# Barriers between the blocks of a two-layer graph network: with and without POOL's drain

## The chip, the cores and the metric

The program runs on one core of one Trainium2 chip. The metric is the device time of one execution in microseconds (us); a lower time is better. Three executions of the kernel before took 2250.91, 2253.52 and 2253.49 us, with a median of 2253.49 us. One more execution was taken with the hardware profiler, and all rows below are from that one.

Engine names as in the profile: PE is TensorE, DVE is VectorE, ACT is ScalarE, POOL is GpSimd, SP is SyncE. A name with a q behind it (POOLq, SPq) is the engine's own instruction queue: it runs waits, semaphore updates, branches and drains, and it hands the engine's work to the engine.

## The reference

A graph has N = 6250 nodes with 128 features each and E = 106250 edges, sorted by receiver. There are two layers, and each adds its result to x and normalises:

```python
# layer 0: an edge network on lengths and directions
w = (silu(silu(emb @ w0 + b0) @ w1 + b1) @ w2 + b2).reshape(-1, 4, 32)
ss, vv = xs[senders], xv[senders]              # gather by edge
mid = products of w, ss, vv and the edge's direction
msg = segment_sum(mid, receivers)              # scatter-add by edge
x = layernorm(x + (msg @ W_out) / 16)
# layer 1: messages by edge type, attention, a GRU-like update
h = relu(concat(x[src], x[dst]) @ W1[type] + b1[type])
m = (h @ W2[type] + b2[type]) * sigmoid(score)
agg = zeros.at[dst].add(m)
x = layernorm(x + layernorm(gru(agg, x) + x))
```

For every edge, one row of a node table is gathered by the edge's sender. That gather is what POOL issues.

## The kernel before, in words

The edges are cut in 104 steps (`STEPS`) of 8 tiles (`TPS`) of 128 edges. The program is a sequence of five blocks (`nc.Block()`). In a block each of the five engines has its own list of instructions, written out by hand, and the engines meet only at semaphores. At the end of a block all engines meet in a barrier.

1. `prepare` (block at line 335): loads inputs, computes keys, edge embeddings and the node table of layer 0 (`node0_d`), and starts the edge network for the first steps. POOL's list ends with the gathers of the first three steps (`gather_step`, line 602, 24 indirect DMAs at line 605), whose landing is not waited for here but in the next block. SP's list ends with 16 stores of the embeddings (line 374) and waits for earlier loads and stores.
2. `edges0` (block at line 717): the 104 steps of layer 0. POOL issues eight gathers per step (`gather_loop`, line 611), first up to four steps ahead of their use and later two (`LEAD_LONG`, `LEAD`). DVE waits for a step's gathers (`landed`), multiplies messages (lines 656 to 672), PE sums them by receiver with one-hot matrices (line 908). Finished nodes are normalised and turned into the tables of layer 1 on the way. Its last part stores the last nodes' tables (line 801), and SP waits for their landing (line 807).
3. `leftover0`, through `run_if_left` (block at line 1172): every engine reads the counter `n_left` (line 1176) and branches (line 1177) over a slow general path. With these inputs the count is zero, so the block is a read, a branch and the barrier.
4. `edges1` (block at line 1531): the 104 steps of layer 1, with the same `gather_loop` on the table `p_tab_d`; at its end the last rows of the output are normalised, POOL computing the last inverse roots (line 1642), and SP stores them (line 1611) and waits for the landing (line 1631).
5. `leftover1`, the same empty block as the third.

The records of a block's barrier carry the line of its `nc.Block()`: on each engine a DRAIN, and then EVENT_SEMAPHORE, which are the barrier's own signals and waits. A DRAIN waits until its engine has finished its work.

The order of work on POOL around the first seam is this:

```python
for u in range(SLOTS - 1):                # end of prepare: steps 0, 1, 2
    e.wait_ge(w["idx_in"][u], 16)
    e.sem_inc(gate, 1)
    gather_step(e, w["idx"], dram["node0"], w["gx"], w["landed"], u)
# barrier of the block at line 335
e.wait_ge(idx_in[SLOTS - 1], 16)          # start of edges0: step 3
e.sem_inc(gate, 1)
gather_step(e, idx, dram["node0"], gx, landed, SLOTS - 1)
gather_loop(e, idx, idx_in, dram["node0"], gx, landed, used, gate, first=1)
```

Of the kernel before, what the change touches and what calls it, by code (L numbers as in the profile page):

```python
# [112 lines left out]
def build(nc, a, out):  # L113

    top = ExitStack()
    with top:
# [27 lines left out]
        with ExitStack() as until_edges1:  # L144
            later.update(between_weights(nc, Mem(nc, until_edges1)))
            with ExitStack() as layer0:
                w = layer0_weights(nc, Mem(nc, layer0))
                nodes = node_views(k, later)
                with ExitStack() as until_leftover0:
                    mlp = first_mlp(Mem(nc, until_leftover0))  # L150
                    prepare(nc, a, k, dram, dict(w, b2_1=later["b2"]), mlp)
                    edges0(nc, a, k, dram, w, later, nodes, mlp)
                leftover0(nc, a, k, dram, w, nodes)
        k["acc_s"] = m.sb("acc_s", [P, NACC])
        edges1(nc, k, dram, later, nodes, out)
        leftover1(nc, a, k, dram, later, out)

# [112 lines left out]
def prepare(nc, a, k, dram, w, mlp):  # L270


    with ExitStack() as ctx:
# [58 lines left out]
        tab_st = m.sems("tab_st", 2)  # L332
        wide_mm, row_clear, centre_ok = (m.sem(n) for n in ("wide_mm", "row_clear", "centre_ok"))

        with nc.Block() as block:

            @block.sync
            def _(e):
# [345 lines left out]
def edges0(nc, a, k, dram, w, later, v, mlp):  # L684

    with ExitStack() as ctx:
# [27 lines left out]
                ps_w[:, 1, 4:8, :].rearrange("p t f -> p (t f)"), ps_w[:, 0, 0:4, :].rearrange("p t f -> p (t f)"),  # L714
                ps_w[:, 1, 0:4, :].rearrange("p t f -> p (t f)")]

        with nc.Block() as block:

            @block.sync
            def _(e):  # L720
# [448 lines left out]
def run_if_left(nc, k, m, layer, plan):  # L1169

    turns = Turns(m.sem("turn"), m.sem("turn_gate"))
    with nc.Block() as block:
        def part(name):
            def run(e):
                flag = e.alloc_register(f"left{layer}_{name}")
                e.load([flag], k["n_left"][0:1, layer:layer + 1])
                with e.If_ne(flag, 0):
                    if name == "sync":
                        e.sem_inc(turns.turn, 1)
                    turns.emit(e, name, plan)  # L1180
            return run
        for name, where in (("sync", block.sync), ("gpsimd", block.gpsimd), ("scalar", block.scalar),
                            ("tensor", block.tensor), ("vector", block.vector)):
            where(part(name))
# [15 lines left out]
def leftover0(nc, a, k, dram, w, v):  # L1200

    with ExitStack() as ctx:
# [79 lines left out]
        def store(e, index):  # L1282
# [24 lines left out]
        ]  # L1307

        run_if_left(nc, k, m, 0, [("vector", lambda e, _: e.memset(k["acc"][:, 0:2 * NACC0], 0.0)), (STEPS, [
            ("sync", load), ("gpsimd", gather),  # L1310
            ("tensor", lambda e, _: e.matmul(ps_h[:], w["w0"][:], emb[:], start=True, stop=True)),
# [11 lines left out]
def leftover1(nc, a, k, dram, w, out):  # L1323

    with ExitStack() as ctx:
# [99 lines left out]
        def product(to, x, y, op):  # L1425
# [27 lines left out]
        ]  # L1453

        run_if_left(nc, k, m, 1, [("gpsimd", lambda e, _: e.memset(k["acc"][:], 0.0)),
                                  ("vector", lambda e, _: e.memset(k["acc_s"][:], 0.0)), (STEPS, [
            ("sync", load), ("gpsimd", gather), ("vector", add_rows),
# [15 lines left out]
def edges1(nc, k, dram, later, nodes, out):  # L1473


    with ExitStack() as ctx:
# [51 lines left out]
        iota_ok = m.sem("iota_ok1")  # L1528
        minus_half, half_ok = m.sb("minus_half1", [P, 2]), m.sem("half_ok1")

        with nc.Block() as block:

            def load_windows(e, regs, j, h):
                for p, start in enumerate(run_starts(e, k, j, regs)):
# [570 lines left out]
```

## Time and profile before

| what | value |
|---|---|
| time, median of three runs (lowest to highest) | 2253.49 us (2250.91 to 2253.52) |
| profiled execution, its own time | 2254.85 us |
| span of the profiled execution | 2253.1 us |
| busy share of the span: PE, DVE, ACT, POOL | 80%, 66%, 60%, 71% |
| mean granted TensorE clock | 0.885 of full |
| DMA traffic | 236.65 MB, mean 105 GB/s |

A row of a timeline gives the start in us from the span's start, the duration in us, engine, line, operation, tiles, count, and in brackets how long the engine was idle before and what ended that. "issue" stands for a pause that nothing in the profile explains. A row of a source line gives the number of instructions, their shortest, median and longest duration in ns, and the start of the first and the last in us.

### The profile page before, as it was taken

The page shows a single profiled execution, that of the slowest core. Times are in us where ns is not written, and L with a number is a line of the kernel's source. Part 1 is how long each engine was busy: PE and PEld are TensorE (multiplying, and loading weights), DVE is VectorE, ACT ScalarE, POOL GpSimd, SP SyncE. Part 2 cuts the span into 40 slices and gives each one's busy share as a digit, 9 for nine tenths or more (in the row PEclk, how much of TensorE's full clock was granted, in tenths as well). Part 3 has the DMA queues.
Part 4 walks back from the last instruction along what each step waited for, and adds up shares of the span by engine and source line. Part 5 has one row for each costly group of instructions (what it writes and reads, how often), then busy time and mean ns, then how long its engine had stood idle before and what let it go on. Part 6 is the DMA issues. An engine that isn't in the chain of part 4 may idle for free. (4 is left out here: it accounts for less than half of the span.)

```text
span 2253.1 us, 43663 instructions
## 1 busy us (share of the span) xinstructions
PE 1810.1 (80%) x10012; PEld 1436.0 (64%) x10012; DVE 1476.7 (66%) x3701; ACT 1347.0 (60%) x4416; POOL 1608.6 (71%) x1699
## 2 busy tenths in 40 slices
PE   7598999999999999999867876766667666676664
PEld 4276666666666766666646766666656666666663
DVE  4566555555655656556546777777777777777775
ACT  2587877777777777777634544544545545454451
POOL 2777777777777777777546777777777777777771
PEclk7599999999999999999979988887887888888886
DMA  6522323323233232333257855445454544544541
GB/s 205 153 54 56 79 74 82 80 72 87 75 82 80 73 85 75 81 80 82 67 168 210 225 118 123 109 118 115 111 122 108 120 115 110 123 109 117 117 110 32
DMA packets 222343, 236.65 MB, mean 105 GB/s; under 512 B 73015, under 2 KB 163295, under 8 KB 222157
## 3 DMA queue, kind: packets, MB, share of 16 engines
q0 software_dynamic: 53808, 112.80, 21.9%
q10 hardware_dynamic: 90012, 58.96, 10.4%
q1 hardware_dynamic: 78481, 64.43, 9.4%
q8 instruction: 14, 0.23, 0.0%
q14 instruction: 28, 0.23, 0.0%
HBM read 191.66 MB, written 44.35 MB: 105 GB/s over the span
## 5 line engine op out<-in xcount | busy, mean ns | idle before, releaser
L605 POOL DMA_INDIRECT gx<-node_d,idx x832 | 798.9, 960 | 265.8 <-issue 259.6
L605 POOL DMA_INDIRECT gp<-p_tab_d,idx x832 | 792.1, 952 | 261.5 <-issue 251.5
L677 ACT ACTIVATE msg<-ws,y 128x32 f32<-128x32 f32 x2496 | 552.8, 316 | 64.5 <-DVE ws L656 64.1
L908 PEld LDWEIGHTS ps_a<-hot,msg 128*128 128x128 f32 x3328 | 408.5, 197 | 194.4 <-issue 113.2
L1754 PE MATMUL ps_e<-win,hot_x 128*128 128x129 f32 x1680 | 300.2, 351 | 272.4 <-DVE hid L1906 249.5
L908 PE MATMUL ps_a<-hot,msg 128*128 128x128 f32 x3328 | 431.8, 285 | 61.5 <-DVE msg L665 40.2
L1754 PEld LDWEIGHTS ps_e<-win,hot_x 128*128 128x128 f32 x1680 | 275.8, 256 | 295.2 <-DVE hid L1906 266.0
L659 DVE TENSOR_TENSOR vy<-gx,y 128x768 f32<-128x768 f32 x104 | 99.6, 958 | 334.1 <-DMA gx<-node_d,idx 334.0
L1655 ACT ACTIVATE hid<-hid,score 128x128 f32<-128x128 f32 x832 | 278.7, 395 | 10.1
L1906 DVE TENSOR_TENSOR hid<-ps_e,gp 128x387 f32<-128x387 f32 (+1 forms) x312 | 142.0, 510 | 147.2 <-DMA gp<-p_tab_d,idx 140.0
L638 PE MATMUL ps_w<-w,h 128*128 128x256 f32 x832 | 221.5, 412 | 0.0
L1818 PEld LDWEIGHTS ps_g<-hot,hid 128*128 128x128 f32 x1664 | 212.9, 200 | 7.7 <-issue 1.1
L1818 PE MATMUL ps_g<-hot,hid 128*128 128x128 f32 x1664 | 212.6, 283 | 0.9 <-ACT hid L1655 0.7
L1651 ACT ACTIVATE score<-hid 128x3 f32<-128x3 f32 (+1 forms) x312 | 61.3, 196 | 245.2 <-DVE hid L1906 240.5
L638 PEld LDWEIGHTS ps_w<-w,h 128*128 128x128 f32 x832 | 158.2, 200 | 67.2 <-issue 48.0
L186 ACT ACTIVATE h<-ps_h,b 128x512 f32<-128x512 f32 x208 | 142.1, 683 | 95.4 <-PE ps_h L191 83.2
L1865 DVE TENSOR_TENSOR hot_x<-key_row,ps_s 128x1024 f32<-128x1024 bf16 x106 | 128.4, 1212 | 32.7 <-PE ps_s L1824 28.2
L1887 DVE TENSOR_TENSOR acc<-acc,ps_g 128x128 f32 x416 | 119.5, 287 | 13.5 <-issue 0.9
L1873 DVE TENSOR_TENSOR hot<-ps_s,key 128x1024 f32<-128x1024 f32 x105 | 127.6, 1215 | 0.0
L1005 DVE TENSOR_TENSOR hot<-ps_a,dloc 128x1024 f32<-128x1024 f32 x104 | 126.6, 1217 | 0.0
L904 PE MATMUL ps_h<-emb,w 16*128 16x512 f32 x202 | 113.2, 640 | 0.0
L191 PE MATMUL ps_h<-h,w 128*128 128x512 f32 x208 | 109.6, 609 | 3.7 <-ACT h L186 3.7
(221 smaller groups left out, 2213.7 us busy)
## 6 DMA issues: line engine op xcount, KB each, us to landing
win<-q_tab_d ACTq DMA_DIRECT2D x416, 64.5 KB
key_row<-key_row_d ACTq DMA_DIRECT2D x102, 256.0 KB, 3.6
gx<-node_d,idx POOLq DMA_INDIRECT x832
gp<-p_tab_d,idx POOLq DMA_INDIRECT x832
p_tab_d<-acc SPq DMA_DIRECT2D x23, 516.0 KB
q_tab_d<-unit_area SPq DMA_DIRECT2D x36, 258.0 KB, 3.3
q_tab_d<-acc SPq DMA_DIRECT2D x5, 774.0 KB, 5.5
emb<-emb_d SPq DMA_DIRECT2D x102, 32.0 KB
```

What stands on the lines that cost most here:

```text
L186: e.activation(mlp[f"h{layer}"][:], mlp["ps_h"][:], ACT.Silu, bias=w[f"b{layer - 1}"][:]).then_inc(ok, 1)
L605: e.indirect_dma_start(out=buf[:, h, t, :], out_offset=None, in_=table, in_offset=bass.IndirectOffsetOnAxis(ap=idx[:, h, t:t + 1], axis=0) ...
L638: last = e.matmul(ps_w[:, 2 * t:2 * t + 2, :], h2[:, t * P:(t + 1) * P], w["w2"][:], start=False, stop=t % 2 == 1)
L677: last = e.activation(self.cols[1][:, tile, c, :], self.ws[:, tile, :], ACT.Copy, scale=y[:, c:c + 1])
L908: last = e.matmul(ps_a[:, h, b, :], msgs[h].tile(t, b), hot[:, h, t, :], start=t == 0, stop=t == TPS - 1)
L1005: e.tensor_tensor(hot[:, h], spread(ps_a[:, h, IOTA, :], 1, TPS), spread(w["dloc"][:, bass.ds(j * TPS, TPS)], 2, P), ALU.is_equal)
L1655: last = e.activation(hid[:, h, t, 0:H], hid[:, h, t, 0:H], ACT.Relu, scale=score[:, h, t:t + 1])
L1754: last = e.matmul(ps_e[:, q, at:at + PW], hot_x[:, h, t, :], win[:, h, t // 2, :], start=True, stop=True)
L1818: e.matmul(ps_g[:, h, t // 2, :], hid[:, h, t, 0:H], hot[:, h, t, :], start=t % 2 == 0, stop=t % 2 == 1)
L1865: e.tensor_tensor(hot_x[:, h].rearrange("p t n -> p (t n)"), key_row[:, h, :], part.to_broadcast([P, TPS * P]), ALU.is_equal).then_inc(hx_ ...
L1873: e.tensor_tensor(hot[:, h], spread(iota[:, 0:P], 1, TPS), spread(k["key"][:, tiles], 2, P), ALU.is_equal).then_inc(hot_ok, 1)
L1906: e.tensor_tensor(hid[:, h, mine, :], ps_e[:, q, 0:n * PW].rearrange("p (t n) -> p t n", t=n), gp[:, u, mine, :], ALU.add).then_inc(pre_ok, 1)
```

## The change

All four places at which a block is opened get one argument; `run_if_left` opens two of the five blocks. By the language's own description, with it the engines other than POOL retire with a plain drain and meet in a barrier made of semaphores alone, and POOL does not drain its queue of descriptors.

```diff
-        with nc.Block() as block:                         # prepare
+        with nc.Block(no_gpsimd_drain=True) as block:
...
-        with nc.Block() as block:                         # edges0
+        with nc.Block(no_gpsimd_drain=True) as block:
...
-    with nc.Block() as block:                             # run_if_left
+    with nc.Block(no_gpsimd_drain=True) as block:
...
-        with nc.Block() as block:                         # edges1
+        with nc.Block(no_gpsimd_drain=True) as block:
```

No other line differs.

## Rows read from the trace of the kernel before

**Rows 1.** Page, parts 1 and 5: busy time; a group, then idle before and releaser

```profile
PE 1810.1 (80%) x10012; PEld 1436.0 (64%) x10012; DVE 1476.7 (66%) x3701; ACT 1347.0 (60%) x4416; POOL 1608.6 (71%) x1699
...
L659 DVE TENSOR_TENSOR vy<-gx,y 128x768 f32<-128x768 f32 x104 | 99.6, 958 | 334.1 <-DMA gx<-node_d,idx 334.0
```

**Rows 2.** Groups on POOL from 95.2 to 1113, 1149 to 2201, and 54 to 95

```profile
L605 POOL DMA_INDIRECT gx<-node_d,idx x808 | 770.9, 954 | 252.3 <-issue 246.1 <-POOLq L335 6.2
...
L605 POOL DMA_INDIRECT gp<-p_tab_d,idx x832 | 792.1, 952 | 261.5 <-issue 251.5 <-DMA idx<-p_idx_d 6.1 <-DVEq L1912 4.0
...
L605 POOL DMA_INDIRECT gx<-node_d,idx x24 | 28.0, 1165 | 13.5 <-issue 13.5
```

**Rows 3.** Timeline of POOL around the first seam

```profile
87.56 0.94 POOL L605 DMA_INDIRECT gx<-node_d,idx  x1 [0.30 <-issue]
88.80 0.94 POOL L605 DMA_INDIRECT gx<-node_d,idx  x1 [0.30 <-issue]
95.99 0.94 POOL L605 DMA_INDIRECT gx<-node_d,idx  x1 [6.24 <-POOLq L335]
```

**Rows 4.** Records of line 335, the barrier of the first block

```profile
L335 POOLq EVENT_SEMAPHORE  x2: 17/17/17, 95.1 to 95.1; - x2
L335 POOLq DRAIN  x1: 23297/23297/23297, 71.7 to 71.7; - x1
L335 ACTq DRAIN  x1: 3376/3376/3376, 81.8 to 81.8; - x1
L335 DVEq DRAIN  x1: 473/473/473, 84.2 to 84.2; - x1
L335 SPq DRAIN  x1: 7/7/7, 85.4 to 85.4; - x1
L335 SPq EVENT_SEMAPHORE  x1: 17/17/17, 95.2 to 95.2; - x1
```

**Rows 5.** Busy time from 85 to 90, from 90 to 95 and from 95 to 100 us

```profile
85.00:90.00 5.00, 0.00 (x0) 0.00 (x0) 0.00 (x0) 0.16 (x1) 3.78 (x4) 0.50 0.69 190
90.00:95.00 5.00, 0.00 (x0) 0.00 (x0) 0.00 (x0) 0.00 (x0) 0.00 (x0) 0.50 0.10 34
95.00:100.00 5.00, 0.46 (x2) 0.46 (x3) 4.53 (x8) 2.51 (x7) 3.40 (x3) 0.50 0.23 47
```

**Rows 6.** Records of line 717, the barrier of the second block

```profile
L717 POOLq DRAIN  x1: 17367/17367/17367, 1100.5 to 1100.5; - x1
...
L717 SPq DRAIN  x1: 7/7/7, 1145.3 to 1145.3; - x1
```

**Rows 7.** Records of line 1172, the barriers of the two empty blocks

```profile
L1172 POOLq EVENT_SEMAPHORE  x4: 17/17/17, 1146.7 to 2253.0; - x4
L1172 PEldq DRAIN  x2: 13/13/13, 1146.5 to 2252.6; - x2
L1172 POOLq DRAIN  x2: 125/129/133, 1146.5 to 2252.6; - x2
```

**Rows 8.** Timelines of POOL and of SP at the end

```profile
1112.05 0.94 POOL L605 DMA_INDIRECT gx<-node_d,idx  x1 [0.30 <-issue]
2199.65 0.95 POOL L605 DMA_INDIRECT gp<-p_tab_d,idx  x1 [0.30 <-issue]
2245.64 0.69 POOL L1642 TENSOR_TENSOR rstd_v<-rstd_v,minus_half 128x2 f32<-128x2 f32 x1 [2.38 <-DVE rstd_v L1936]
...
2246.74 0.36 SPq L1611 DMA_DIRECT2D out<-unit_area  x1
```

**Rows 9.** Records of line 1531, the barrier of the fourth block

```profile
L1531 POOLq EVENT_SEMAPHORE  x2: 17/17/17, 2251.7 to 2251.8; - x2
...
L1531 POOLq DRAIN  x1: 6031/6031/6031, 2245.6 to 2245.6; - x1
L1531 DVEq DRAIN  x1: 386/386/386, 2246.4 to 2246.4; - x1
...
L1531 SPq DRAIN  x1: 7/7/7, 2248.6 to 2248.6; - x1
```

**Rows 10.** Timelines of POOL and DVE from 97 to 163: long gathers, first and last

```profile
97.24 1.54 POOL L605 DMA_INDIRECT gx<-node_d,idx  x1 [0.31 <-issue]
102.83 1.20 POOL L605 DMA_INDIRECT gx<-node_d,idx  x1 [0.30 <-issue]
121.88 1.53 POOL L605 DMA_INDIRECT gx<-node_d,idx  x1 [0.30 <-issue]
162.50 1.65 POOL L605 DMA_INDIRECT gx<-node_d,idx  x1 [0.30 <-issue]
...
121.64 0.95 DVE L659 TENSOR_TENSOR vy<-gx,y 128x768 f32<-128x768 f32 x1
```

## The prediction

> **What bounds the kernel now.** I read the page's busy shares first: PE is busy for 80% of the span, POOL for 71% [rows 1]. By that PE looks like the bound. The idle time speaks otherwise: DVE's first operation of each of the 104 steps of layer 0 waits for its gathers, 334 us in all [rows 1]. So I looked next at POOL's groups by stretch. From 95.2 to 1113 us POOL issues 808 gathers of 954 ns, and its idle time is 246 us of "issue", about 0.30 us behind each gather, and one wait of 6.2 us for POOLq at line 335. It waits for nothing else. In layer 1 the 832 gathers take 952 ns each, with 251.5 us of "issue" and only 10 us of other waits [rows 2]. One gather costs 1.25 us from start to start, one step 10.0 us, and both layers run at that pace. Whatever moves POOL's chain of gathers moves the end of a layer by as much.
>
> Then the seams. The only hole in POOL's chain in layer 0 is between the gather that starts at 88.80 and the one at 95.99 [rows 3]; line 335 is a block's barrier. The other two places at which POOL's drain can matter are the seam between the layers and the end.
>
> **First seam, the gain on POOL.** POOL's last gather of the first block ends at 88.80 + 0.94 = 89.74. Its DRAIN began at 71.7 and took 23.297 us, so it ended at 95.0 [rows 4]: 5.26 us after the last gather. The signals follow at 95.1 and 95.2, and the next gather starts at 95.99. Without the drain nothing holds it but its own place in line: 89.74 + 0.30 = 90.04. POOL gains 95.99 - 90.04 = 5.95 us.
>
> For this the barrier must open early enough. The DRAIN's record begins at 71.7, when the gathers that start at 87.56 and 88.80 were still to come [rows 3, 4]. So POOL's queue runs well ahead of its engine. Without a drain it gives its signal near 71.7, and the barrier waits for the others: ACT to 81.8 + 3.4 = 85.2, DVE to 84.7, SP to 85.4. It opens about 85.5, when POOL still has three or four gathers in hand. After the old barrier the queue needed from 95.1 to 95.99, some 0.9 us, to bring the next gather; from 85.5 that is 86.4, and 90.04 stays the limit. If POOL's signal waited for its last gather after all, the next would start at 89.74 + 0.99 (the time from 95.0 to 95.99) = 90.73, and the gain would be 5.26. I take 5.9 and keep 5.3 as the lower end.
>
> The Trainium skill, page "PSUM — Partial Sum Buffer", section "Engine vs sequencer instructions", says that an increment on a sequencer's instruction behind engine work can fire while that work is in flight, since the sequencer waits only until it is handed over. By that rule POOL signals before its gathers end and the gain is 5.9; by the opposite reading 5.3. The record that begins at 71.7 [rows 4] agrees with the rule.
>
> **First seam, the others.** DVE, ACT, PE and SP start at about 85.5 instead of 95.2, 9.7 us earlier. I count none of it as gain, because POOL's gathers set the pace [rows 2]. It costs nothing either, as far as the cover goes. DVE's first three steps have been gathered or are being gathered; SP's first index loads go out ten us earlier, and POOL needs the first of them only after the eight gathers of step 3, at 90.04 + 10.0. The DMA engines are 0.69 busy from 85 to 90 and 0.10 from 90 to 95 [rows 5]; SP's loads of embeddings and weights wait behind the stores of that first stretch and then fill the empty one. Were the loads late, POOL's cover is 10 us minus some 3 us of landing.
>
> One side effect has a price. Where DVE works beside POOL a gather can take longer: 1.54 and 1.20 us right after the seam, and 1.53 to 1.65 us once per step in six steps from 121.88 to 162.50, each where DVE runs line 659 [rows 10]. That is 0.6 us each, in the time in which DVE catches up with a backlog. The last four gathers of the first block, free of it now, will stand beside DVE: one more such gather, +0.6. On the other hand DVE gains 9.7 us and POOL 5.9, so the backlog is 3.8 us smaller; at 8.1 us per step ((162.50 - 121.88)/5) against POOL's 10.0 that is two steps less of catching up, -1.2. I take zero, and -1.2 to +0.6 for the range.
>
> **Seam between the layers.** POOL's drain runs from 1100.5 to 1117.9, 4.9 us beyond its last gather (1112.05 + 0.94), but SP reaches the barrier only at 1145.3 [rows 6, 8]: 27 us of cover, gain zero. In the empty block behind it POOL's DRAIN takes 0.13 us, at the same time as PE's at 1146.5; the signals go at 1146.7 [rows 7]. I take zero, and -0.2 to +0.2, one record's length on either side, since a barrier of semaphores alone is not in this trace. The same bound for each of the other barriers makes ±0.4 over all.
>
> **End.** POOL's last operation ends at 2245.64 + 0.69 = 2246.33, SP's last store goes out at 2246.74 [rows 8]. SP has waited for its landing and is at the barrier at 2248.6; POOL's DRAIN lasts from 2245.6 to 2251.6, the barrier opens at 2251.7, and the rest to 2253.1 is the last empty block [rows 9, 7]. Without the drain SP is last: 2251.6 - 2248.6 = 3.0 us gained. The stall's place is taken by the store's landing, which stays.
>
> **Sum.** 5.9 + 0 + 3.0 = 8.9 us. The profiled execution took 2254.85 us, 1.75 above its span, so it would take 2245.9; its span would be 2244.2. It stood 1.36 us above the median of the runs, so the median becomes 2253.5 - 8.9 = 2244.6 us, 0.4% less. The terms' bounds give -10.9 (5.95 + 3.0 + 1.2 + 0.4, and rounding) to -6.9 (5.3 + 3.0 - 0.6 - 0.4, less rounding): 2242.6 to 2246.6.
>
> **Rival 1: the price comes back after the program.** The drain's length does not depend on what is in flight. The last gather started at 2199.65, yet at the end POOL's drain lasts 5.3 us beyond POOL's last operation; after 808 gathers it was 4.9, after 24 it was 5.26. Only a drain with no gather since the one before is short, 0.13 us [rows 4, 6 to 9]. So it is a fixed price, owed once gathers have been issued. With the change no drain is left, and if what closes an execution has one of its own, it pays. The program ends 3.0 us earlier, then 5.3 are paid: +2.3 at the end, -5.9 at the first seam, 2253.5 - 3.6 = 2249.9. For it speaks the fixed price; against it that only 1.75 us of the time lies outside the span, start included. The Trainium skill speaks on both sides. Page "VectorE: DVE Perf Modes", section "The DRAIN you can't avoid", tells of drains in the runtime's preamble and postamble on all five engines, of about 12 ns; by that figure the debt costs nothing, by this kernel's rows 5.3 us. No row here shows these drains. Chance 0.13.
>
> **Rival 2: the change does not do what it says.** POOL would still be waited for, by a drain under another name or one that the barrier needs: 2253.5. Against it speaks that the other engines' records are separate from POOL's and as short as 7 ns [rows 4]. Chance 0.09.
>
> **Rival 3, slower: the engines fall out of step.** DVE starts 9.7 us earlier and POOL 5.9, so their phase changes, and the collisions of [rows 10] could stay through the layer. Place: line 605 beside line 659. Price: 0.6 us per step, since POOL's chain is the bound. It outweighs the gain from 8.9 / 0.6 = 15 further steps; over half of the 104 steps it is +31, so 2275. For it: six steps in a row did collide. Against it: they stopped at 162.50, when the backlog was gone and DVE's start hung on the landings, and over the layer the mean is 954 ns [rows 2]. Chance 0.05.
>
> **How the numbers follow.** The forecast has 0.70; 0.03 is for a larger gain, such as earlier work in layer 1 by luck of timing. Three runs of one kernel lie 2.6 us apart, so about 0.2% (4.5 us, below 2249.0) is what can be told from no change. Faster: 0.70 + 0.03 + 0.04, the lower side of rival 1 = 0.77. Within 0.2%: the other 0.09 of rival 1 and most of rival 2 = 0.17. Slower: 0.06. The range goes from 2241.0 (2242.6, less the runs' scatter) to 2250.5, which takes in rival 1 and leaves rivals 2 and 3 out.
>
> **What would show it.** In the new profile there is no DRAIN on POOLq at the blocks' lines; the gather behind 88.8 starts 0.30 us after its end, near 90.0; DVE's first work of layer 0 is near 85.7; SP's record at line 1531 and the end of the span are 1.4 to 1.5 us apart in place of 4.5; the gathers' mean stays at 0.95 us; the first gather of layer 1 starts 5.9 us earlier, near 1143.4. Rival 1 shows as time outside the span, far above 1.75 us. The prediction is wrong if a hole of 5 us opens elsewhere on POOL, if POOL begins to wait for index loads or for DVE, or if long gathers appear in many steps.

## The result, and the profile after

| | before | after |
|---|---|---|
| median of five runs (lowest to highest) | 2250.91 us (2249.43 to 2253.52) | 2238.56 us (2234.61 to 2240.77) |
| profiled execution, its span | 2254.85 us, 2253.1 us | 2238.56 us, 2236.8 us |

The ratio of the runs is 0.9938, with a 95% interval of 0.9923 to 0.9953: the changed kernel is faster by 12.4 us by the medians, and by 10.6 to 17.3 us by the interval times 2250.9. The forecast was 8.9 us less and 2244.6 us, with 2241.0 as the low end. The direction was right. The time is 6.0 us below the forecast and below the range. Of these 6.0 us, 2.6 lie in the start of the sum (2253.49 was taken for the kernel before, and its five runs here have 2250.91) and 3.4 in the gain (12.4 in place of 8.9).

The page of the changed kernel, parts 1 and 5, in the columns of [rows 1]:

```profile
PE 1800.7 (81%) x10012; PEld 1429.1 (64%) x10012; DVE 1476.3 (66%) x3701; ACT 1342.2 (60%) x4416; POOL 1605.7 (72%) x1699
...
L605 POOL DMA_INDIRECT gx<-node_d,idx x832 | 797.8, 959 | 259.7 <-issue 259.4
L605 POOL DMA_INDIRECT gp<-p_tab_d,idx x832 | 790.3, 950 | 260.8 <-issue 249.1
L659 DVE TENSOR_TENSOR vy<-gx,y 128x768 f32<-128x768 f32 x104 | 99.5, 957 | 324.8 <-DMA gx<-node_d,idx 324.7
```

The busy times have hardly moved. POOL's gathers still have no idle time but "issue", and DVE still waits for them in each step of layer 0. The 6.2 us behind POOLq at line 335 [rows 2] are gone.

The timeline of POOL in the changed kernel around the first seam; the gather that starts at 83.65 is the 24th, the last of the first block (88.80 in [rows 3]):

```profile
82.40 0.95 POOL L605 DMA_INDIRECT gx<-node_d,idx  x1 [0.30 <-issue]
83.65 0.95 POOL L605 DMA_INDIRECT gx<-node_d,idx  x1 [0.30 <-issue]
84.90 0.94 POOL L605 DMA_INDIRECT gx<-node_d,idx  x1 [0.30 <-issue]
```

Records of line 335 in the changed kernel, to be read against [rows 4]:

```profile
L335 ACTq EVENT_SEMAPHORE  x2: 17/17/17, 79.1 to 79.3; - x2
L335 POOLq EVENT_SEMAPHORE  x2: 17/17/17, 79.1 to 79.2; - x2
L335 ACTq DRAIN  x1: 3365/3365/3365, 75.7 to 75.7; - x1
...
L335 SPq DRAIN  x1: 7/7/7, 78.3 to 78.3; - x1
```

There is no DRAIN on POOLq. The barrier opens at 79.2, when the last of the others, ACT, has drained (75.7 + 3.4). POOL then has four gathers of the first block still to issue, and issues them without a pause: the hole of 7.19 us from start to start has become 1.25, a gather's normal distance. DVE's first work of layer 0 starts at once, at 79.91, the time in us at the head of this row of its timeline:

```profile
79.91 0.43 DVE L1112 COPY ps_a<-iota 128x256 f32<-128x256 f32 x1 [1.74 <-PEq L335]
```

Records of lines 717, 1172 and 1531 in the changed kernel, the later barriers [rows 6, 7, 9]:

```profile
L717 POOLq EVENT_SEMAPHORE  x2: 17/17/17, 1133.8 to 1133.9; - x2
...
L717 SPq DRAIN  x1: 7/7/7, 1133.7 to 1133.7; - x1
...
L1172 POOLq EVENT_SEMAPHORE  x4: 17/17/17, 1135.2 to 2236.7; - x4
...
L1531 POOLq EVENT_SEMAPHORE  x2: 17/17/17, 2235.3 to 2235.3; - x2
...
L1531 SPq DRAIN  x1: 7/7/7, 2235.2 to 2235.2; - x1
```

At line 717 SP was last before (1145.3) and is last now (1133.7). At line 1531 SP drains at 2235.2 and the barrier opens 0.1 us later; before it waited 3.0 us more for POOL.

Timelines of POOL, with the last gather of each layer and its last operation, and of SP, with the last store [rows 8]:

```profile
1100.27 0.94 POOL L605 DMA_INDIRECT gx<-node_d,idx  x1 [0.30 <-issue]
2185.69 0.94 POOL L605 DMA_INDIRECT gp<-p_tab_d,idx  x1 [0.30 <-issue]
2232.20 0.69 POOL L1642 TENSOR_TENSOR rstd_v<-rstd_v,minus_half 128x2 f32<-128x2 f32 x1 [2.38 <-DVE rstd_v L1936]
...
2233.30 0.36 SPq L1611 DMA_DIRECT2D out<-unit_area  x1
```

One point after the other, the 16.3 us between the two profiled executions come from these places:

| point | before, us | after, us | after minus before | gained in this stretch |
|---|---|---|---|---|
| first gather starts | 54.77 | 50.20 | -4.57 | 4.57 |
| 24th gather | 88.80 | 83.65 | -5.15 | 0.58 |
| 25th gather (first seam) | 95.99 | 84.90 | -11.09 | **5.94** |
| last gather of layer 0 | 1112.05 | 1100.27 | -11.78 | 0.69 |
| last gather of layer 1 | 2199.65 | 2185.69 | -13.96 | 2.18 |
| last store | 2246.74 | 2233.30 | -13.44 | -0.52 |
| last barrier but one opens | 2251.7 | 2235.3 | -16.4 | **2.96** |
| end of the span | 2253.1 | 2236.8 | -16.3 | -0.1 |

The two bold stretches are the two places of the forecast. They give 5.94 + 2.96 = 8.9 us, the forecast's sum. The other 7.4 us lie where the two kernels do the same (2.4 of them in layer 1 itself, whose first gather moved from 1149.31 to 1137.72), and 4.57 of them were gained before any barrier had been reached. So the question for the experiments was: is that luck of one execution, or something else that the missing drain brings? Before them I held the first; the rival was a gain of 3 us or more beside the seams.

### The profile page after: what moved, and what is told of

The parts are those of the page before. It is cut to its first block and busy times, and to the rows that moved or that the text cites. A ratio compares the mean times of both kernels' runs of the same rounds, so it can differ in the third digit from the quotient of the medians.

```text
span 2236.8 us, 43678 instructions
## 1 busy us (share of the span) xinstructions
PE 1800.7 (81%) x10012; PEld 1429.1 (64%) x10012; DVE 1476.3 (66%) x3701; ACT 1342.2 (60%) x4416; POOL 1605.7 (72%) x1699
```

## The experiments

Times are medians in us. A ratio compares all comparable runs of a kernel with those of the kernel before on the same chip. "Mean" is the difference of the two means, with its standard error worked out from the runs' spread.

| kernel | drain left out at | its median | before (runs) | ratio and its 95% interval | mean |
|---|---|---|---|---|---|
| e1_first_only | 335 | 2995.38 | 2982.18 (35) | 1.0044, 1.0019 to 1.0069 | +14.0 ± 3.4 |
| e2_end_only | 1531 | 2985.9 | same | 1.0002, 0.9973 to 1.0031 | +1.4 ± 3.6 |
| e3_middle_only | 717, 1172 | 2984.45 | same | 1.0008, 0.9986 to 1.0029 | -0.1 ± 2.3 |
| e4_same | none | 2987.1 | same | 1.0001, 0.9978 to 1.0023 | -0.1 ± 2.7 |
| e5_after | all | 2237.3 | 2247.4 (26) | 0.9956, 0.9937 to 0.9974 | -10.6 ± 1.3 |
| e6_first_only | 335 | 2239.79 | same | 0.9967, 0.9952 to 0.9983 | -6.8 ± 1.4 |
| e7_end_only | 1531 | 2247.9 | same | 1.0004, 0.9987 to 1.002 | +1.7 ± 1.5 |
| e9_not_empty | 335, 717, 1531 | 2251.79 | 2248.5 (29) | 1.0012, 0.9997 to 1.0027 | +2.8 ± 1.4 |
| e11_not_first | 717, 1172, 1531 | 2242.58 | same | 0.9984, 0.9968 to 1.0 | -5.1 ± 1.4 |
| e12_after | all | 2238.43 | same | 0.9953, 0.9938 to 0.9968 | -10.3 ± 1.5 |
| e13_warm_after | all, more matmuls | 2235.87 | 2245.73 (20) | 0.9953, 0.9937 to 0.9968 | -10.6 ± 1.3 |
| e14_after | all | 2237.93 | same | 0.9961, 0.9947 to 0.9975 | -8.2 ± 1.4 |
| e15_warm_before | none, more matmuls | 2242.09 | same | 0.9984, 0.997 to 0.9997 | -3.4 ± 1.3 |

### One place at a time, on a chip on which POOL is not the bound

Each of the first kernels has the argument at one place only (line 335; line 1531; lines 717 and 1172), and e4_same is the kernel before:

```diff
-        with nc.Block() as block:             # line 335 alone (e1_first_only)
+        with nc.Block(no_gpsimd_drain=True) as block:
```

> Only the block of prepare (line 335) ends without POOL's drain. Theory A (the drain's price is paid at two seams, 5.9 us at the first and 3.0 us at the end, and the rest of the measured 12.4 us is not the change's): 5.9 us less than before, and in the profile 1.25 us between the 24th and the 25th gather where before has 7.19. Theory B (taking the drain away at the first seam is worth more than the hole, since the other engines start 9.7 us earlier and the backlog is smaller): 8 to 10 us less, with fewer long gathers in layer 0 or a shorter layer 1. Theory C (the first 50 us of the program, which gave 4.6 us in the profiled execution, become shorter with the change): the first gather starts near 50 us and not near 54.8.

> Only the block of edges1 (line 1531) ends without POOL's drain. Theory A: 3.0 us less than before, the barrier of line 1531 opening 0.1 to 0.2 us after SP's DRAIN record, the time outside the span unchanged at 1.75 us. Rival, the price comes back after the program: the span is 3.0 us shorter but the time outside it grows to 4 us or more. If the missing 3.5 us of the whole change are to be found here, 6 us less.

> Only edges0 (line 717) and the two empty blocks (line 1172) end without POOL's drain. Theory A: no difference, within 0.5 us: POOL's drain of line 717 is long over when SP arrives, and those of line 1172 take 0.13 us. Theory B': a drain in the middle has a later cost, such as a slower start of layer 1's gathers: 1 to 4 us less, with the first gather of layer 1 closer to the barrier than the 2.4 us of before.

> The kernel before, nothing changed, as a measure of chance. Theory A and chance: ratio 1.000, but the first gather, which started at 54.8 us before and at 50.2 us after, starts somewhere between these in a new profiled execution, according to the granted TensorE clock between 25 and 60 us. Theory C: it starts near 54.8 us, and the clock there is 0.5 again.

Nothing became faster. For e3_middle_only and e4_same that was expected. For e2_end_only the 3.0 us expected are within an error of ± 3.6, and its trace shows why they need not come: the DRAIN of the last empty block takes 5.355 us there, as in e7_end_only below. The clear miss is e1_first_only. The trace of e4_same, the unchanged kernel, shows how this chip differs. It takes 2987.1 us here, and these are three of its four longest waits (engine and line, waited for, us in total, times, longest):

```profile
DVE ws L656 <- remote: 542.3, 73, 17.3
POOL gx L605 <- DVEq L1093: 328.0, 74, 16.9
POOL gp L605 <- DVEq L1912: 266.3, 66, 14.7
```

The trace of before has no wait of POOL for DVE of that size; in layer 1 it is 4.0 us [rows 2]. Here POOL waits 594 us for DVE to free the buffers, so POOL is ahead and its seam is covered. DVE is not the bound either: it is busy for 50% of the span and itself waits 542 us for "remote", the view's word for another core or a queue that it can't name. What bounds the kernel on this chip is open. The run bears on what the forecast hangs on: where POOL did not set the pace, closing the hole at the first seam brought no gain. In e1_first_only the hole was gone (1.25 us from the 24th to the 25th gather, 5.39 in e4_same) and the time did not fall. Why this chip is 33% slower, and why e1 was even 0.44% slower than before there, is left open; in its profile 52.7 us lie between the last gather of layer 0 and the first of layer 1, against 44.9 in e4_same, and in that stretch DVE waits 13.7 us and ACT 10.3 for "remote". No experiment was made on that.

### The same on a chip like that of the forecast

> The whole change again. On the chip of the runs e1 to e4 the kernel before took 2982 us, and POOL waited there for DVE in both layers (328 and 266 us); taking the first drain away closed the hole behind the 24th gather (1.25 us between starts) without a gain. Theory A: where the kernel before takes about 2250 us, POOL's gathers are the bound and the change gives 8.9 us and up to 14; where it takes about 2980 us, they are not, and only the 3.0 us at the end are left, 0.1%, inside the noise. Rival: 12 us less on either kind of chip.

> As e1: only the block of prepare ends without POOL's drain. Theory A, where the kernel before takes about 2250 us: 5.9 us less. Theory B: 8 to 10 us less. Theory C (the start of the program is shorter): the first gather near 50 us instead of 54.8. Where the kernel before takes about 2980 us: within 0.4% of it, either sign.

> As e2: only the block of edges1 ends without POOL's drain. Theory A: 3.0 us less where the kernel before takes about 2250 us. If the missing 3.5 us are to be found here: 6 us less. By the profile the barrier of line 1531 opens 0.1 to 0.2 us after SP's DRAIN record, and the time outside the span stays 1.7 us; the rival of the postponed price has it at 4 us or more.

The whole change gives 10.6 ± 1.3 us on this chip. The first seam alone gives 6.8 ± 1.4 us by the means (3.8 to 10.8 by the ratio's interval), which holds the 5.9 of the forecast, but the 8 to 10 of theory B as well. In the profile of e6_first_only the timeline of POOL has no hole; these are the 23rd, 24th and 25th gather:

```profile
86.69 0.95 POOL L605 DMA_INDIRECT gx<-node_d,idx  x1 [0.30 <-issue]
87.94 0.94 POOL L605 DMA_INDIRECT gx<-node_d,idx  x1 [0.30 <-POOLq L335]
89.19 0.94 POOL L605 DMA_INDIRECT gx<-node_d,idx  x1 [0.30 <-issue]
```

The end alone gives nothing (+1.7 ± 1.5 us), where the forecast's term says -3.0. Records of lines 1172 and 1531 of e7_end_only show why (durations in ns as shortest, median and longest, then the starts in us):

```profile
L1172 POOLq DRAIN  x2: 132/2744/5355, 1146.4 to 2246.0; - x2
...
L1531 SPq DRAIN  x1: 7/7/7, 2245.0 to 2245.0; - x1
```

The barrier at line 1531 opens at 2245.2, 0.2 us behind SP, as it should. But now the DRAIN of the last empty block takes 5.36 us in place of 0.13 [rows 7]. The price had only been passed on, and since it starts later, it costs more: from SP's drain to the end of the span it is 2251.6 - 2245.0 = 6.6 us, against 4.5 before. That is rival 1's mechanism, inside the program.

### What the drain's price depends on

The prediction called it a fixed price, owed once gathers have been issued. Two kernels put small blocks between the layers, behind the first `run_if_left`; they are a measurement of drains, and their time is not compared. In e8_small_blocks four blocks hold one operation of POOL each (a memset, one gather, a memset, one plain DMA), and each waits for what it issued. In e10_ladder seven blocks hold 2 to 64 gathers:

```diff
+        for n in (2, 4, 8, 16, 24, 32, 64):
+            with nc.Block() as block:
...
+                    for t in range(n):
+                        if t and t % TPS == 0:
+                            e.wait_ge(landed, 16 * (done + t))
+                        e.indirect_dma_start(...).then_inc(landed, 16)
+                    e.wait_ge(landed, 16 * (done + n))
```

> The kernel before with four small blocks between the third and the fourth, all ending with POOL's drain: POOL does in them one memset; one indirect gather whose landing it waits for; one memset; one direct DMA whose landing it waits for. The theory (the drain has a fixed price, owed once POOL has issued a DMA since the last drain, and not for what is in flight): POOL's DRAIN records take 0.1 to 0.2 us in the first and third block and 4.5 to 5.5 us in the second and fourth. Rival 1 (the price grows with the number of DMAs): about 0.2 us in all four. Rival 2 (the price belongs to any work after a while): 5 us in all four. Rival 3 (only the indirect kind has it): 5 us in the second alone.

> The kernel before with seven blocks more behind the third, all ending with POOL's drain. In them POOL issues 2, 4, 8, 16, 24, 32 and 64 gathers and waits for the landing of all before the block ends. One gather so treated left a DRAIN of 0.13 us, 832 of them one of 5.3 us. If the price grows with the number of gathers since the last drain up to a limit: DRAIN records rising from about 0.2 us to about 5 us, level from some number on. If it does not depend on the number but on being behind a loop or on a long time: all seven near 0.13 us. If it is a step between one and many: 5 us from 2 on.

Records of the drains of e8_small_blocks, behind a memset and behind one gather:

```profile
L166 POOLq DRAIN  x1: 40/40/40, 1139.6 to 1139.6; - x1
...
L171 POOLq DRAIN  x1: 133/133/133, 1144.4 to 1144.4; - x1
```

One gather costs 0.13 us, not 5.3: the fixed price is refuted. (The empty blocks' drains take 0.12 to 0.13 us behind no gather at all [rows 7], so at one gather the price can't be told from theirs.) Records of three of the drains of e10_ladder, behind 2, 24 and 64 gathers:

```profile
L166 POOLq DRAIN  x1: 210/210/210, 1156.9 to 1156.9; - x1
...
L166 POOLq DRAIN  x1: 2002/2002/2002, 1238.4 to 1238.4; - x1
...
L166 POOLq DRAIN  x1: 5274/5274/5274, 1382.9 to 1382.9; - x1
```

The seven drains took 0.210, 0.368, 0.695, 1.348, 2.002, 2.655 and 5.274 us behind 2, 4, 8, 16, 24, 32 and 64 gathers. That is 0.05 us plus 0.082 us per gather, (5.274 - 0.210) / 62. All gathers had landed by then, so what is paid for is not their transfer. Behind 832 gathers it is 5.3 to 5.4 us (e7, e9): the price grows no further somewhere from 64 on.

In the kernel before, 24 gathers lie behind line 335, and there the drain lasted 5.26 us beyond the last one instead of 2.0. Those had not all landed. Busy time of two stretches of the kernel before, in the columns of [rows 5] (the last two numbers are the busy share of the DMA engines and GB/s), shows when they had:

```profile
93.00:93.25 0.25, 0.00 (x0) 0.00 (x0) 0.00 (x0) 0.00 (x0) 0.00 (x0) 0.50 0.04 16
93.25:95.00 1.75, 0.00 (x0) 0.00 (x0) 0.00 (x0) 0.00 (x0) 0.00 (x0) 0.50 0.00 0
```

The last data move before 93.25, and the drain ends at 95.0. In all nine profiles with the drain at line 335 it ends 3.5 to 5.9 us beyond the last gather on POOL, but always 1.7 to 1.9 us behind the last packets of the gathers' DMA queue. So here the drain does wait for what is in flight. That its 5.26 us looked like the 5.3 at the end is chance, and it is 3.5 in e4_same and e11_not_first. The 1.7 to 1.9 us left are near the 2.0 of 24 landed gathers. How the two parts add up is open: the drain of line 717, behind 808 gathers more, also ends only 2.0 us behind the queue's last packets in the kernel before, and not 5.3.

### Which barriers have to go together

e9_not_empty leaves the drain in the empty blocks alone, e11_not_first at line 335 alone; e12_after is the changed kernel.

> The change at three of its four places: the two empty blocks (line 1172) keep POOL's drain. Theory A (each place has its own gain): as the whole change, 8.9 us less than before. Theory D (a drain that is left out is owed, and the next drain pays it, about 5.3 us from its own start): POOL's DRAIN of the first empty block takes about 5 us where it took 0.13, with nothing beside it, +5.0; that of the last one 5.4 us, as in the run with the change at the end alone, +2.1 against before; with -5.9 at the first seam the kernel is 1.2 us slower than before, within 3 us either way.

> The complement of the run with the first block alone: the drain stays at prepare (line 335) and goes at the other three places. Theory A and theory D agree here, as no drain is left behind the last one that goes: 3.0 us less than before, the end of the span 1.5 us behind SP's DRAIN record of line 1531 where before has 4.5. If the gain at the end were lost to work after the program, no difference and more than 1.8 us outside the span.

> The whole change once more, beside its three parts on one chip. Theory D: 8.9 us less than before by the trace of the kernel before; with the hole at the first seam as other traces of before show it (4.1 to 6.6 us gained there) 7 to 10 us less. If more than luck stood behind the 12.4 us of the first comparison: 12 us less again.

Records of line 1172 of e9_not_empty:

```profile
L1172 POOLq DRAIN  x2: 5368/5374/5379, 1138.3 to 2243.9; - x2
```

Both empty blocks now pay for the layer before them, at places where nothing runs beside them. Between the layers the old drain had 27 us of cover; here its 5.4 us lie on the path. By the terms this is -5.9 at the first seam, +5.3 between the layers and +2.1 at the end, +1.5 in all; measured +2.8 ± 1.4. So three of four places without the drain bring no gain, and by the traces a small loss. e11_not_first brings the end's term alone, 5.1 ± 1.4 us against 3.0: in its trace SP drains at 2239.0 and the span ends at 2240.6, 1.6 us later, as in the changed kernel.

### Where the rest of the first comparison came from

In ten profiles on ordinary chips the start of the first gather falls into two heaps: 53.2 to 55.6 us (before, e6, e7, e10) and 49.6 to 51.4 (after, e5, e8, e9, e11, e12). It is ahead of any barrier, and kernels with the drain at line 335 are in both (e8 and e11 early). What goes with it is TensorE's granted clock. e13_warm_after and e15_warm_before keep TensorE busy in its idle stretch ahead of 25 us, with 24 matmuls that nothing reads, in the changed kernel and in the one before:

```diff
                     if s == 0:
                         e.wait_ge(row_clear, 1)
+                        for _ in range(24):
+                            e.matmul(ps_b[2][:, 0:P], w_up[:], w_up[:], start=True, stop=True)
                         e.wait_ge(ld_wide, 16)
```

> The changed kernel with 24 matmuls of 128x128 more on PE, whose result nothing reads, in the idle stretch from about 19 to 25 us ahead of the wait for the wide loads. Theory A (the start's spread comes from TensorE's granted clock): the clock from 30 to 40 us is 0.8 or more in the profile, the first gather starts at 49.5 to 51 us, and the runs are on average 2 to 3 us faster than e14_after (it is high in part of its executions already; 4.6 us at most), with fewer late runs among the five. Theory B (the clock is a companion, and the spread comes from loads or from the chip): the first gather still falls between 49.6 and 55.6, the time is that of e14_after within 1 us; the added matmuls may also make the start later, by up to 3 us. If the clock stays at 0.50 from 30 to 40 us all the same, the test says nothing on A. Against the kernel before: -11 to -13 us by A, -9 to -10 by B.

> The changed kernel once more. Theory (seams alone): 8.9 us less than the kernel before, with a scatter of some 3 us between comparisons, so 6 to 12. Rival (something besides the seams gains 3 us more): again 12 us or more, as in the first comparison.

> The kernel before with the same 24 matmuls. Theory A: 2 to 3 us faster than the kernel before, first gather at 49.5 to 51 us. Theory B: same as before within 1 us, or up to 3 us slower. In both theories e15 minus e13 is the drain's effect with the start's spread taken out, 8.9 us; a rival that the drain left out also helps the clock would make it 12.

Busy time from 20 to 50 us, in the columns of [rows 5] (the third number from the right is the granted clock), for the kernel before, the changed kernel, e14_after, e13_warm_after and e15_warm_before, one fence each:

```profile
20.00:50.00 30.00, 24.80 (x59) 14.43 (x60) 10.49 (x14) 9.00 (x13) 2.71 (x5) 0.56 0.60 201
```

```profile
20.00:50.00 30.00, 23.91 (x68) 12.34 (x68) 10.57 (x14) 11.75 (x17) 2.70 (x5) 0.69 0.58 202
```

```profile
20.00:50.00 30.00, 25.63 (x60) 14.75 (x61) 10.49 (x14) 9.64 (x13) 2.70 (x5) 0.55 0.58 204
```

```profile
20.00:50.00 30.00, 28.77 (x102) 17.25 (x101) 10.50 (x14) 11.02 (x16) 2.70 (x5) 0.70 0.59 204
```

```profile
20.00:50.00 30.00, 28.14 (x100) 16.93 (x99) 10.49 (x14) 11.45 (x17) 2.81 (x6) 0.73 0.58 205
```

Beside the first gather's start the clocks read:

| | before | after | e14 | e13 | e15 | e5, e12, e11, e8, e9 | e6, e7, e10 |
|---|---|---|---|---|---|---|---|
| clock, 20 to 50 us | 0.56 | 0.69 | 0.55 | 0.70 | 0.73 | 0.71, 0.72, 0.67, 0.69, 0.66 | 0.56, 0.52, 0.53 |
| first gather, us | 54.77 | 50.20 | 53.88 | 50.24 | 49.89 | 50.54, 49.63, 49.73, 50.59, 51.40 | 54.23, 55.59, 53.23 |

Two heaps again, and nothing between them. On the slow chip the clock and the start do not go together so well: e4_same has 0.73 from 20 to 50 us and starts at 53.15 all the same. e14_after settles the rival: it is the changed kernel, letter for letter, and starts as late as the kernel before, at the low clock. The added matmuls went with an early start in both kernels. The place can be seen at PE's first matmuls of line 568 (570 in the warm kernels) come after its idle stretch. PE's timeline in the changed kernel and in e15_warm_before:

```profile
24.32 2.04 PE L568 MATMUL ps_h<-acc,of_row 16*128 16x512 f32 x2 [5.78 <-DMA acc<-length_d]
```

```profile
24.82 1.12 PE L570 MATMUL ps_h<-acc,of_row 16*128 16x512 f32 x2 [1.19 <-DMA acc<-length_d]
```

After 5.78 us of idleness the pair takes 2.04 us, at a granted clock of 0.50, the lower of the two levels (1.2 GHz); after 1.19 us it takes 1.12, at 1.00, the higher one (2.4 GHz). In the changed kernel the clock came back in time in most profiles, in the kernel before in fewer; with a dozen profiles in all that is no difference between the two. The expectation of a clock of 0.8 or more from 30 to 40 us missed in e13 (0.59; it had 1.00 from 20 to 30). On the average of the runs the matmuls bring 2.4 ± 1.4 us in the changed kernel (2238.3 to 2235.9) and 3.4 ± 1.3 in the one before: the 2 to 3 us that theory A expected, 2.9 ± 1.0 together. Two early starts in two profiles would prove little, since 6 of the other 11 were early too; the means are the evidence.

e14_after also shows a seam that is not quite free. POOL's timeline from its 23rd gather on (the first column is the start):

```profile
86.69 0.94 POOL L605 DMA_INDIRECT gx<-node_d,idx  x1 [0.30 <-issue]
87.94 0.94 POOL L605 DMA_INDIRECT gx<-node_d,idx  x1 [0.30 <-issue]
89.72 0.94 POOL L605 DMA_INDIRECT gx<-node_d,idx  x1 [0.84 <-issue]
```

SP drained at 88.7 there, the barrier opened at 88.9, and the next gather came 0.8 us later, 0.54 us late. That is the prediction's "0.9 us after the barrier" at work. Since a gather comes 0.30 us behind the one before in any case, POOL pays once the barrier opens less than some 0.6 us before its last gather ends; here it opened at 88.9, when that gather ended.

The first seam's hole, over all profiles, was 5.4 to 7.8 us with the drain (5.39 in e4, 7.84 in e3) and 1.24 to 1.78 without, so the term is worth 4 to 6.6 us by execution. On the ordinary chips the hole with the drain was 6.5 to 7.7 us in the three late starts (before, e7, e10) and 5.4 to 6.0 in the three early ones (e8, e11, e15). The mean of the six is 6.4 us, that of the seven without the drain 1.4, so the first seam is worth 5.1 us on average, and the execution from which the prediction took its 5.9 was one with a longer hole.

Five comparisons now measure the whole change by means: 14.0 ± 1.5 (the first), 10.6 ± 1.3, 10.3 ± 1.5, 8.2 ± 1.4, and e15 against e13, 7.2 ± 1.3 (both with the start held early). Weighted by their errors they give 9.9 ± 0.6 us, and without the first 9.0 ± 0.7. The forecast's 8.9 is within that scatter, 1.6 errors below the mean of all. The five differ among themselves by more than their errors allow (14.0 and 7.2 are 6.8 ± 2.0 apart), so 0.6 is too small an error for their mean. The last of them fits the traces: the hole was 5.76 us in e15 and 1.68 in e13, which with 3.0 at the end makes 7.1 us. Whether the last microsecond is real stays open.

e13_warm_after has the lowest median of all, 2235.87 us, below the kernel before by the ratio in the table; against e14_after on the same chip its 2.4 ± 1.4 us are a likely gain, not a sure one.

## Why the prediction was wrong in its number

**What bounds the kernel: right** on three of the four chips of the experiments. On the other one POOL waited 594 us for DVE, what bounds it is open, and the first seam gave no gain.

**First seam: right in this pair of executions.** 5.94 us measured, 5.95 worked out; over all profiles of ordinary chips it is 5.1 on average. The queue ran ahead: POOL's signal was out by 79.1, with gathers in hand until 85. The Trainium skill, page "PSUM — Partial Sum Buffer", section "Engine vs sequencer instructions", says that a sequencer's instruction can fire while the engine's work is in flight; the rows of line 335 agree. DVE's start came at 79.9 and not at 85.7, since it follows the barrier, and this execution had started early.

**Cover and collisions: right in sum.** POOL waited for no index load worth naming (0.3 us for DVE over 808 gathers). From the 25th gather to the last of layer 0 it is 1016.06 us before and 1015.37 after. Over all profiles of ordinary chips it is 1014.3 to 1021.5 with the first drain (six, mean 1016.6 ± 1.2) and 1011.8 to 1018.0 without (seven, mean 1014.6 ± 1.0): 2.0 ± 1.5 us, which could be the last microsecond above, or nothing. Rival 3 asked for +31.

**Seam between the layers: right.** Zero gained; SP is last in both, and from the last gather of layer 0 to the first of layer 1 it is 37.26 us before and 37.45 after.

**End: right in size**, 2.96 us, but only since the empty block lost its drain as well. The prediction priced the places one by one and summed them. e7 and e9 show that they aren't independent: the last drain left behind pays for all the gathers before it.

**Rival 1: right as a mechanism, wrong in its place.** Time outside the span was 1.75 us before and 1.76 after, and 1.68 to 1.80 in the other kernels of the ordinary chips. So nothing was paid after the program. The Trainium skill, page "VectorE: DVE Perf Modes", section "The DRAIN you can't avoid", tells of about 12 ns for drains outside a kernel's own work; those are not in our traces, but the outside time leaves no room for 5.3 us. POOL's drains inside the program are far above that figure, 0.13 to 5.4 us once gathers have been issued. The reason given for the rival, a fixed price that "does not depend on what is in flight", fell with e8, e10 and the packets ahead of the first seam. **Rival 2** is refuted by the absent records of POOL's DRAIN.

**The step that failed is the last one**: "so the median becomes 2253.5 - 8.9 = 2244.6 us", and the range's low end of "2242.6, less the runs' scatter", with "three runs of one kernel lie 2.6 us apart". It took the median of three runs for the kernel's time and their spread for its scatter. (The terms' bounds add up to -10.55 and -7.3; the 0.35 and 0.4 us of rounding on top have no working, and don't change the picture.) 75 runs of the kernel before on three ordinary chips lie between 2238.83 and 2256.97 us, with medians of 2247.4, 2248.5 and 2245.73 and a standard deviation of 4.0 to 4.5 us on each chip. Against these the three runs stood about 6 us high, and even the five of the comparison 2 to 5, while the changed kernel's 2238.56 is within 1.3 us of its medians elsewhere (2237.3, 2238.43, 2237.93). 2247.2 less 8.9 would have been 2238.3. Whether the high runs were chance or belong to their chip was not tried. Part of that scatter was in the profile: the granted clock of 0.50 from 30 to 50 us, ahead of the first gather, goes with a start about 4 us later (54.3 against 50.4 on the means of the two heaps), and the profiled execution from which I took the rows was one of the late starts. With 4 us per run, a median of three on one side and of five on the other differ by some 3.6 us by chance (1.25 x 4 us, over the roots of 3 and 5, added in squares). A range for 8 times in 10 takes 1.3 of these, 4.7 us, below the forecast and then the terms' own bounds: its low end is near 2238, not 2241. The two terms came out near their size, the first of them by one execution's luck as much as by its reasoning; the anchor, 2253.5, and its error did not.

## What to carry to other kernels

Price a drain by what its queue has issued since the last one, by what is still in flight, and by what ends beside it. A drain that is left out is paid by the next one that is left in. That does no harm where the next one is covered (e6_first_only: the drain of line 717 has 27 us of cover) and eats the gain where nothing covers it (e7_end_only, e9_not_empty), so behind the last gather leave it out at every barrier or at none. A gain at a seam is worth its length only if the engine that waits there sets the pace on the chip at hand. And before a gain of a few microseconds is put beside a median, ask how far single runs of the same kernel scatter, and look for a clock or another state in the profile that could have gone the other way.

## What the runs showed of the hardware

- POOL's DRAIN took 0.034 to 0.040 us behind a memset, 0.12 to 0.13 behind one DMA, and behind n indirect gathers that had landed 0.05 + 0.082 n us up to 64 (5.27 us), no more than 5.4 behind 832. A drain left out is owed to the next one. With gathers still in flight (line 335) it ended 1.7 to 1.9 us behind their queue's last packets, in nine profiles of nine.
- One chip ran the same program in 2982.18 us instead of 2247, at a mean granted clock of 0.79 instead of 0.89, with DVE and ACT waiting for "remote" (DVE 542 us at line 656, ACT 296 us at line 186). By the ratio of the clocks alone it would be at most 13% slower, not 33%; the cause is open.
- On one ordinary chip (26 runs of the kernel before) a run was 9.7 us shorter for each 0.01 of mean granted clock more, with a correlation of -0.84. On the other two it was 6.8 us with -0.55 (29 runs) and 12.8 us with -0.79 (20 runs). Which of the two follows the other was not tried, except at the start.
